# Two graph layers on one core: mirrored edge tiles converted by GpSimd, row work spread over iterations, no-edge rows by a tiny added row, turns between the attention products

## The reference

```
h = relu(layernorm(x))
cos = beta * (h @ h.T) / (norm(h) @ norm(h).T + 1e-7)
P = softmax(cos + (1 - adj) * -1e9, axis=1)
x = x + P @ h
h = relu(layernorm(x))
deg = max(sum(adj, axis=1), 1)
x = x + h @ W_self + ((adj @ h) / deg) @ W_neigh
```

## Time and profile before

| | us |
|---|---|
| median of 3 runs | 538.41 (537.03 to 540.01) |
| the profiled execution's own time | 538.77 |
| its span from first to last instruction | 537.0 |

### The profile page before, as it was taken

How to read it: one execution, slowest core, us unless ns; L and a number is a source line. 1 busy time by engine, 2 the same in 40 slices (tenths; PEclk the granted TensorE clock), 3 DMA queues, 4 the chain that set the end, 5 groups by cost and what they waited for, 6 DMA issues and landing times.

```text
span 537.0 us, 12656 instructions
## 1 busy us (share of the span) xinstructions
PE 474.5 (88%) x5336; PEld 407.1 (76%) x5336; DVE 323.2 (60%) x745; ACT 325.0 (61%) x459; POOL 265.7 (49%) x221
## 2 busy tenths in 40 slices
PE   0066999999899998999899989887979999999996
PEld 0043888988789877887788778666768988888895
DVE  6873696557766469665985695784983332321353
ACT  2769887787597796979688968858643111101111
POOL 2846777666467665676577756847553000000000
PEclk9977999999899999999999999988989999999999
DMA  8414767667564675657736736452110010000001
GB/s 235 156 40 153 241 218 224 207 199 226 178 201 128 229 244 195 195 177 222 251 114 222 250 130 222 166 176 81 60 32 4 1 40 1 21 21 21 21 1 40
DMA packets 31548, 74.38 MB, mean 139 GB/s; under 512 B 2560, under 2 KB 15104, under 8 KB 31488
## 3 DMA queue, kind: packets, MB, share of 16 engines
q1 hardware_dynamic: 31488, 73.54, 42.9%
HBM read 71.43 MB, written 2.10 MB: 137 GB/s over the span
## 4 chain that ended last, share of the span: by engine, by line
PE 68%; DVE 14%; ACT 7%; issue 5%; POOL 2%; DMA 1%; SPq 1%; DVEq 0%; ACTq 0%; POOLq 0%
PE ps L1037 21%; PE ps L915 13%; PE ps L926 9%; PE ps L976 4%; PE ps L973 4%; PE ps L975 4%; PE ps L953 3%; DVE word L758 3%; PE ps L950 3%; PE ps L952 3%; ACT word L532 3%; DVE far L776 3%; DVE x_sb L714 2%; ACT ps L533 2%; PE ps L1023 2%
## 5 line engine op out<-in xcount | busy, mean ns | idle before, releaser
L389 POOL TENSOR_TENSOR near<-word,adj_t 128x1024 f32<-128x1024 f32 x72 | 144.9, 2013 | 121.6 <-PE ps L976 60.7
L532 ACT ACTIVATE word<-ps,small 128x512 f16<-128x512 f32 x144 | 134.9, 937 | 76.4 <-PE ps L915 76.1
L915 PE MATMUL ps<-unit_t 128*128 128x512 f16 x432 | 142.8, 391 | 7.7 <-DVE word L758 4.4
L758 DVE TENSOR_TENSOR word<-ps,word 128x512 f16<-128x512 f32 x144 | 101.1, 735 | 40.6 <-ACT ps L533 40.3
L926 PE MATMUL ps<-ident,word 128*128 128x128 f32 x448 | 107.7, 282 | 18.9 <-DVE word L758 18.9
L1037 PE MATMUL ps<-table,adj_t 128*128 128x257 f16 x1024 | 117.0, 274 | 0.0
L776 DVE TENSOR_TENSOR far<-ps,adj_t 128x1024 f32<-128x1024 f32 x56 | 68.5, 1223 | 72.7 <-PE ps L926 72.7
L1037 PEld LDWEIGHTS ps<-table,adj_t 128*128 128x128 fp8e4 x1024 | 99.2, 98 | 13.3 <-POOL table L423 0.3
L973 PE MATMUL ps<-table,near 128*128 128x129 f16 x576 | 105.1, 222 | 3.1 <-POOL near L389 3.1
L533 ACT ACTIVATE ps<-ps,small 128x512 f32<-128x512 f32 x144 | 106.7, 741 | 0.0
L976 PE MATMUL ps<-table,near 128*128 128x129 f16 x576 | 105.4, 225 | 0.0
(11 more groups left out here) (95 smaller groups left out, 512.7 us busy)
## 6 DMA issues: line engine op xcount, KB each, us to landing
stage<-in_adj_dram SPq DMA_DIRECT2D x128, 512.0 KB, 4.3
x_sb<-in_x_dram SPq DMA_DIRECT2D x4, 512.0 KB, 6.3
x_again<-in_x_dram SPq DMA_DIRECT2D x8, 256.0 KB, 4.8
out_dram<-x_sb SPq DMA_DIRECT2D x7, 256.0 KB, 2.3
out_dram<-x_sb SPq DMA_DIRECT2D x1, 192.0 KB, 2.0
stage<-in_L_gnn_W_neigh_dram SPq DMA_DIRECT2D x1, 64.0 KB, 2.8
stage<-in_L_gnn_W_self_dram SPq DMA_DIRECT2D x1, 64.0 KB, 2.2
out_dram<-x_sb SPq DMA_DIRECT2D x1, 64.0 KB, 1.5
```

The source lines that it names most:

```text
L389: pool.tensor_tensor(ring(near, k), ring(word, k), adj_t[:, near_adj(k)], ALU.mult).then_inc(s_near, 1)
L532: act.activation(half(word16, k, c, 0, HIGH, TPS), score(k, c), ACT.Exp, bias=exp_bias, scale=exp_scale)
L758: dve.tensor_tensor(half(word16, k, c, 0, LOW, TPS), score(k, c), half(word16, k, c, 0, HIGH, TPS), ALU.subtract).then_inc(s_elo, 1)
L915: ins = pe.matmul(score(k, c), j, rows, start=i == 0, stop=i == 2)
```

## The change

- The far tiles are converted by GpSimd (`convert_far`), behind the conversion of the near tile of the same pair; ScalarE's `convert` goes.
- On TensorE the scores of pair k+2 come first, then far attention k, then the turns of pair k+1, then near attention k (in a near-only iteration near attention precedes the turns). Before, turns and scores were interleaved.
- On VectorE an iteration is now: first low part of pair k+2, spill, second low part, far mask of pair k+1. The evacuation stands ahead of that in a step's first iteration, new rows in the second, statistics in the third, scales in the fourth.
- `pair_order` places the two near-only pairs of a step among the far ones, as its third and fifth pairs, and not at its end.
- Rows without edges: `no_edge`, the sum of h times 2^-100 with 4096 x 2^-100 as its denominator, is added to every row when a bank is first evacuated or spilled; the flag, the mean's copy, the four reductions, the mixings and the loop's fp32 products go. The sum of h is taken in the opening by 32 fp32 products (`sum_of_h`).
- Opening: GpSimd's first three conversions move behind the inverse norms; the eight `table_high` come after the exps of the first eight pairs; `low_parts` follow the near masks 0, 2, 4 ...; TensorE computes the scores of pair 0 after the third group of unit transposes, and PSUM banks are reassigned for that.
- The later `scales_of_x2`, `second_h` and `second_low` stand at other iterations.

```diff
+            def convert_far(k):
+                m = FAR_BEFORE[k]
+                slot = 2 + m % 2
+                pool.wait_ge(s_far_in[m % 2], (m // 2 + 1) * 16)
+                if k == FIRST[2]:
+                    pool.wait_ge(s_tab, NS)
+                    pool.wait_ge(s_mean, 1)
+                pool.tensor_scalar(far_adj(k, adj_tb), stage[:, slot * TILE:(slot + 1) * TILE].rearrange("p (t c) -> p t c", t=TPS),
+                                   FP8_ONE, 0.0, ALU.mult, ALU.add).then_inc(s_adjt, 1)
...
             inverse_std(0)
-            convert(0)
             inverse_std(1)
-            convert(1)
             inverse_std(2)
...
-            convert(2)
-            low_parts(0)
-
+            convert(0)
             pool.wait_ge(s_max, 1)
...
+            convert(1)
+            convert(2)
+            convert_far(2)
...
                 mask_near(k)
+                if s == 0 and k % 2 == 0:
+                    low_parts(k // 2)
                 if k + LEAD < NP:
                     convert(k + LEAD)
-                if s == 0 and k % 2 == 0 and k // 2 + 1 < NS:
-                    low_parts(k // 2 + 1)
-                if 1 <= s <= 6 and at == 4 - s // 6:
-                    scales_of_x2(s - 1)
-                if 1 <= s <= 5 and at == 7 - s // 5 * 2:
-                    second_low(s - 1)
+                    if PAIR[k + LEAD][2]:
+                        convert_far(k + LEAD)
+                for done in range(NS - 2):
+                    if k == FIRST[done + 1] + 4:
+                        scales_of_x2(done)
+                    if k == FIRST[done + 1] + 8:
+                        second_low(done)
...
                     exps(k, general)
-                    if k + 2 < NP and PAIR[k + 2][2]:
-                        convert(k + 2)
-                    if s == 0 and k < 4:
-                        table_high(4 + k)
-                    if 1 <= s <= 5 and at == 6 - s // 5:
-                        second_h(s - 1)
-                        second_high(s - 1)
+                    if k < NS:
+                        table_high(k)
+                    for s in range(NS - 3):
+                        if k == FIRST[s + 1] + 6:
+                            second_h(s, 0, 2)
+                        if k == FIRST[s + 1] + 7:
+                            second_h(s, 2, TPS)
+                            second_high(s)
...
+            dve.wait_ge(s_hsum, 1)
+            dve.tensor_scalar(no_edge[:, 0:D], ps[:, transpose_bank(NS - 1), 0:D], TINY, None, ALU.mult).then_inc(s_mean, 1)
...
-                        dve.tensor_copy(rows, two_rows(acc_bank(s, b))).then_inc(s_evac, 1)
+                        dve.tensor_tensor(rows, two_rows(acc_bank(s, b)), no_edge_two, ALU.add).then_inc(s_evac, 1)
...
-                then(dve.tensor_scalar(den_s, x_v3[:, s * TPS:(s + 1) * TPS, D], HS, 1e-30, ALU.mult, ALU.max))
+                then(dve.tensor_scalar(den_s, x_v3[:, s * TPS:(s + 1) * TPS, D], HS, None, ALU.mult))
                 then(dve.reciprocal(rden, den_s))
-                dve.tensor_scalar(ne_p, den_s, 1e-30, 1.0, ALU.is_le, ALU.mult)
...
-                for t in range(TPS):
-                    row = x_row(s * TPS + t)
-                    last = dve.scalar_tensor_tensor(row, mean_h[:, :], ne_p[:, t:t + 1], row, ALU.mult, ALU.add)
-                last.then_inc(s_mixed, 1)
...
                     if s >= 1 and at == 0:
                         evacuate(s - 1)
+                    if s >= 1 and at == 1:
+                        new_rows(s - 1)
+                    if s >= 1 and at == 2:
+                        done = row_stats(s - 1)
+                    if s >= 1 and at == 3:
+                        row_scales(s - 1, done)
+                    if k + 2 < NP:
+                        if general:
+                            scale_scores(k + 2, 0)
+                            scale_scores(k + 2, 1)
+                        low_part(k + 2, 0)
+                    if PAIR[k][2]:
+                        spill(k)
+                    if k + 2 < NP:
+                        low_part(k + 2, 1)
                     if k + 1 < NP and PAIR[k + 1][2]:
                         mask_far(k + 1)
-                    if k + 2 < NP:
-                        words(k + 2, general)
-                    if PAIR[k][2]:
-                        spill(k)
-                    if s == 0 and 3 <= k < 3 + TPS:
-                        partial_sum(k - 3)
-                    if s >= 1 and at == 0:
-                        new_rows(s - 1)
-                    if s >= 1 and at == 1:
-                        done = row_stats(s - 1)
-                    if s >= 1 and at == 2:
-                        row_scales(s - 1, done)
...
+            sum_of_h(0, T - TX)
+            unit_transpose(0)
+            unit_transpose(1)
+            sum_of_h(T - TX, T)
+            unit_transpose(2)
+            pe.wait_ge(s_ulo, 2)
+            scores(0)
+            unit_transpose(3)
+            unit_transpose(4)
+            unit_transpose(5)
+            unit_transpose(6)
+            pe.wait_ge(s_mean, 1)
+            unit_transpose(7)
+            pe.wait_ge(s_ulo, 3)
+            scores(1)
             pe.wait_ge(s_ulo, NS)
             pe.wait_ge(s_first, 5)
-            scores_and_turns(0, NP)
-            scores_and_turns(1, NP)
             for k in range(NP):
-                scores_and_turns(k + 2, k + 1)
+                if k + 2 < NP:
+                    scores(k + 2)
                 if PAIR[k][2]:
                     attend_far(k)
-                attend_near(k)
-                if k == 10:
-                    mean_products()
+                else:
+                    attend_near(k)
+                if k + 1 < NP and PAIR[k + 1][2]:
+                    turns(k + 1)
+                if PAIR[k][2]:
+                    attend_near(k)
...
-    order = [(s, p, p // 2 > s) for s in range(steps)
-             for p in ([*range(pairs)] if s == 0 else [*range(2 * s + 2, pairs), 2 * s, 2 * s + 1])]
+    order = []
+    for s in range(steps):
+        own, later = [2 * s, 2 * s + 1], [*range(2 * s + 2, pairs)]
+        at = 0 if s == 0 else min(2, len(later) - 1) if later else 0
+        mine = own + later if s == 0 or not later else later[:at] + own[:1] + later[at:at + 1] + own[1:] + later[at + 1:]
+        order += [(s, p, p // 2 > s) for p in mine]
```

99 lines of the change are left out of this document (38 added, 61 removed).

## The result

| | before | after |
|---|---|---|
| median, us | 537.72 (536.85 to 540.01), 4 runs | 518.13 (517.82 to 519.28), 4 runs |
| the profiled execution's own time, us | 538.77 | 518.36 |
| its span, us | 537.0 | 516.5 |

The ratio is 0.963, with an interval of 0.960 to 0.967: the kernel is 19.6 us faster.

A forecast was written before the change was run, and what follows sets the result against it. TensorE was taken as the bound, with time to be had only where it idles or runs at a lower clock. -1.5 - 0.9 - 12.5 - 1.35 + 1.7 = -14.6 took 538.8 to 524.2 us, range 515 to 533.5.

The forecast's parts named there:

- steady far iterations: Attention loop: TensorE keeps the same four items, so an iteration with a far tile stays at 4.92 us.
- GpSimd doesn't become the bound: Rival denied: far conversions in GpSimd's queue make all engines fall to its pace, 547 us, chance 0.07.
- r: Duration of a far conversion on GpSimd in the loop: 1.05 to 1.2 us, 1.1 taken.
- 0.3 us of slack of the far mask: Plain far iterations: VectorE's mask ends 0.3 us before far attention is due; rival that it is late: 536.2, chance 0.07.
- Four terms of the sum: Sum's terms in us: opening -1.5, mean products -0.9, step changes -12.5, tail -1.35, turns apart from scores +1.7.
- Opening: Up to iteration 4: moved conversions bring unit rows about 2 us sooner; -1.5 us taken, range -3.5 to +2.0.
- the opening gives nothing: Rival: scores ahead of transposes on a half-clock TensorE delay unit rows 3 to 7, +2.0 for -1.5; 527.7 us, chance 0.09.
- Mean products and turns apart: Loop on TensorE: eight mean products leave, -0.9 us; 56 turn sets apart from scores cost 0.03 each, +1.7, bounds 0 to +3.9.
- Step changes: Five changes between steps lose 25.5 us before and 2.6 each after: -12.5 us.
- the 1.1 end: Upper bound per step change for row updates held up by GpSimd, 0.5 taken; as a rival 527.2 us, chance 0.12.
- two waits of 1.05 on the far mask: Each step change: after each near-only iteration far attention waits 1.05 us for VectorE's mask, 2.1 together.
- Tail: First iteration of step 6 to the end of attention, 23.44 us before: -1.35 us, bounds -2.7 and -0.7.

The follow-up runs named there:

- e5: Changed kernel with the 128x4 flag and four mixings put back on VectorE in new rows: 531.00 us, ratio 0.988.
- e12: Changed kernel with both old queue orders, turns between score products on TensorE and far mask first on VectorE: 521.18 us, ratio 0.970.
- e8: Changed kernel with GpSimd converting far tiles in step 0 only and ScalarE those of later steps: 516.15 us, ratio 0.962.
- e1: Changed kernel with ScalarE converting all far tiles again instead of GpSimd: 519.34 us, ratio 0.970.
- e7: Changed kernel with the scores of pair 0 after the last group of unit transposes, not after the third: 515.27 us, ratio 0.960.
- e6: Changed kernel with GpSimd's first two conversions of the opening back between the inverse deviations: 520.44 us, ratio 0.968.
- e2: Changed kernel with the two near-only pairs at the end of a step, as before: 520.08 us, ratio 0.971.
- e4: Changed kernel with VectorE's far mask ahead of the second low part in near-only iterations followed by a far one: 517.68 us, ratio 0.967.
- e11: Changed kernel with the edits of e7, e8 and e4, plus the four row updates split two and two over two iterations: 516.78 us, ratio 0.961.

## Why the prediction was right or wrong

**Right.** That TensorE bounds the kernel and only its idle stretches can give time; steady far iterations stayed at 4.92. That GpSimd doesn't become the bound: r was 1.05, the low end of 1.05 to 1.2, because an operation of four pieces costs GpSimd nothing more than a flat one. That the 0.3 us of slack of the far mask hold in plain iterations: no waits there. That most of the gain is at the step changes and comes from VectorE's queue (e5 gives 10.3 of the 14.4 us back, e12 another 3.6). Four terms of the sum had the wrong size; all errors but the tail's lay on the same side. Of the signs, ScalarE's busy time fell by 52 us and not by 60, one wait of 1 us on the far mask came per step and not two, and the clock of the opening, which was not to be under 0.8, was 0.87 from 36 to 62 us but 0.72 from 30 to 36.

**Opening: 4.1 instead of 1.5.** Of the 2.6 that the forecast lacked, 1.7 is the chain's (iteration 4 at 62.16, not 63.9) and 0.9 is that the text took only 1.5 of the 2.4 that its own chain gave, for fear of the clock. The chain had the low part at about 32.7, and TensorE went on at 31.29: VectorE's chain up to the unit rows was 1.4 us shorter than I had added up. The half clock for the scores was right for this profile but wrong for seven others, in which the first exp came another 1.7 us sooner. So the opening's own size is nearer to 6 us than to 4: e8, with the same instructions, is at iteration 4 at 60.15. The text names the four table parts that ScalarE sheds ahead of its first exp. It never prices by themselves the far conversions that ScalarE sheds in the first iterations, which e1 and e8 put at 3.7 us. That the early scores delay was the ground of a rival (the opening gives nothing), and e7 bears the ground out, though not the rival: the early scores cost some 2.7 us, less than the moved conversions (1.8, e6) and ScalarE's relief (3.7, e8 against e1) bring. The rest of the opening's gain was not separated.

**Mean products and turns apart: 0.9 saved, nothing paid; 1.7 was booked.** Eight turns take 0.88 us in a block where they took 0.87 between scores; the lower bound was right, and 0.03 for each of 56 was a guess with no row.

**Step changes: 14.4 instead of 12.5.** Before lost 26.3 us between iterations 4 and 66 (309.6, less 0.9 for the mean products, less 52 far iterations of 4.92 and 10 near-only ones of 2.66), not 25.5. After lost 11.9 by the same account, 2.4 per step change, where 2.6 was booked. That near hit hides two errors. New rows took 4.2 us and not 2.55, since a small operation and the updates wait for GpSimd; that is even beyond the 1.1 end of what I had given them, and TensorE then waits 1.07 for words. (Undisturbed, new rows take 1.7 us, as at 382.44 in after, so the 2.55 must already have held one delay like the 1.21, and the 0.5 on top of it was in part booked twice.) But I added this to two waits of 1.05 on the far mask. Waits in a row don't add: after TensorE has waited 1.07 for words, the far mask of the next iteration, which would have been 1.05 late, is only 0.2 late. The second wait (0.98) came as the text said.

The Trainium skill, SBUF — State Buffer, section "Who interferes with whom", says that a VectorE operation with two SBUF inputs contends with a GpSimd operation that reads SBUF, and that the port between them is an exclusive lock. The traces agree for the row updates, 2.45 us here and 4.39 in the tail for 1.14. The same section of the Trainium skill says that a copy or a scalar operation of VectorE can take the shared port too. The 1.60 and 1.83 us of the 128x4 operations agree with that.

**Tail: 0.75 instead of 1.35,** at the lower bound. The walk gave the row updates of step 5 an ordinary length; they took 4.39 us, nearly four times 1.14, and far attention 68 came 2.9 late. The 0.75 is luck besides: the same instructions took 25.5 us in e6 and 24.3 in e7, longer than the 23.4 of before, and with such a tail the term would have had the wrong sign.

**What the text didn't separate.** It booked the step changes as one term. e5, e12, e2 and e1 split it: the removed mixing 10.3 us, the two queue orders 3.6, the placing of near-only pairs 1.6, the far conversions on GpSimd -1.4. These last bring 3.7 in the opening instead. A reader of my part by part could have thought the new order did it; the walk never asked what the old order would lose without the mixing.

## What to carry to other kernels

Where a saturated engine waits at a recurring place, list what stands in the late engine's queue there and take work out before reordering it: 1.9 us of row work taken out of each step change gave 10 us over five of them, the clock's part included, while reorderings at the same place (e4, e11) moved the wait or made it grow. Orders on two engines that wait for each other are one edit: one half of this one without the other costs 57 us, the whole gains 4. When a walk finds several waits in a row, carry the delay forward, and don't add them. And before reading a small difference from two profiles, look how far a stretch repeats where the instructions are the same: here 0.04 us in the middle of the kernel, and almost 3 us in its tail.

## What the runs showed of the hardware

- VectorE's smallest operations are the dearest beside GpSimd: a 128x4 scalar operation or copy of 0.15 to 0.17 us took 1.60, 1.83 and 1.84 us, and four row updates took 1.14 us undisturbed, 2.45 beside two conversions and 4.39 beside a mask, a conversion and a table part in a row. An elementwise engine that gets more work lengthens another's operations even where neither is the bound (674 against 547 ns for a row update, 1.4 us over five step changes).
- A GpSimd conversion whose rows come in four pieces costs as much as a flat one (1052 and 1049 ns).
- Eight fp32 turns back to back take 0.88 us at a granted clock of 1.00, as much as between score products (0.87).
- The same opening ran its six scores in 2.4 us in one profile and in 1.3 in another, at a granted clock of 0.72 and 1.00 for that stretch. The tail's same instructions took 22.7, 24.3 and 25.5 us in three profiles, at clocks of 1.00, 0.93 and 0.88. One profile of a stretch after idle time is not enough to price it.
